# The messages of the tensor-product layer inside the first 100 turns of the ODE loop

## What is computed

```python
tpw = h @ W_mlp4 / jnp.sqrt(jnp.float32(W_mlp4.shape[0]))   # h: 64 numbers an edge
w1, w2, w3, w4 = jnp.split(tpw, 4, axis=-1)
s0 = x0[sender]; s1 = x1[sender]
p1 = w1 * s0 * y0
p2 = (w2 * s0)[:, :, None] * y1[:, None, :]
p3 = w3[:, :, None] * s1 * y0[:, None, :]
p4 = w4 * jnp.einsum('eum,em->eu', s1, y1) / SQRT3
msg0 = jax.ops.segment_sum(jnp.concatenate([p1, p4], axis=-1), receiver, num_segments=num_nodes)
msg1 = jax.ops.segment_sum(jnp.concatenate([p2, p3], axis=1), receiver, num_segments=num_nodes)
```

```python
f = lambda z: _mlp(z, *params)           # tanh, tanh, linear
k1 = f(y)
k2 = f(y + dt / 2 * k1)
k3 = f(y + dt / 2 * k2)
k4 = f(y + dt * k3)
return y + dt * (k1 + 2 * k2 + 2 * k3 + k4) / 6
```

## Time and profile before

| | |
|---|---|
| median of 3 runs | 7954.03 us (7952.38 to 7956.33) |
| the profiled execution | 7959.73 us |
| its span | 7958.1 us |
| TensorE busy | 6785.0 us, 85% of the span, 208683 matmuls |
| VectorE busy | 2457.7 us, 31% |
| ScalarE busy | 1713.8 us, 22% |
| GpSimd busy | 697.0 us, 9% |

### The profile page before, as it was taken

How to read it: one execution, slowest core, us unless ns; L and a number is a source line. 1 busy time by engine, 2 the same in 40 slices (tenths; PEclk the granted TensorE clock), 3 DMA queues, 4 the chain that set the end, 5 groups by cost and what they waited for, 6 DMA issues and landing times. The chain is left out here.

```text
span 7958.1 us, 480626 instructions
## 1 busy us (share of the span) xinstructions
PE 6785.0 (85%) x208683; PEld 3933.2 (49%) x208683; DVE 2457.7 (31%) x12720; ACT 1713.8 (22%) x7668; POOL 697.0 (9%) x1191
## 2 busy tenths in 40 slices
PE   7889989999999999999888888888888888888741
PEld 5423244444444444444487555555555555555520
DVE  5257643211111111111133222222222222222247
ACT  0223222333333333333100111111111111111111
POOL 0034359200000000000000000000000000000000
PEclk9889989999999999999899999999999999999975
DMA  1133211000000000000032111111111111111100
GB/s 42 22 85 89 79 53 50 8 0 0 0 0 0 0 0 0 0 0 0 12 120 71 6 6 6 6 7 6 6 6 6 6 6 7 7 6 6 20 12 7
DMA packets 739824, 152.53 MB, mean 19 GB/s; under 512 B 694067, under 2 KB 708981, under 8 KB 739756
## 3 DMA queue, kind: packets, MB, share of 16 engines
q1 hardware_dynamic: 695596, 85.27, 7.2%
q0 software_dynamic: 40704, 45.90, 2.1%
q10 hardware_dynamic: 3456, 20.48, 0.6%
HBM read 123.19 MB, written 28.16 MB: 19 GB/s over the span
## 5 line engine op out<-in xcount | busy, mean ns | idle before, releaser
L988 PE MATMUL ode_busy<-ode_busy_x,ode_busy_w 128*32 128x320 f16 (+2 forms) x40000 | 2344.2, 311 | 44.5 <-issue 37.6
L1461 PE MATMUL ps_rows<-whh,h_pair 128*4 128x384 f16 x34944 | 1554.1, 327 | 149.7 <-DVE h_pair L1361 146.1
L1461 PEld LDWEIGHTS ps_rows<-whh,h_pair 128*4 128x4 f16 x34944 | 746.1, 84 | 774.0 <-DVE h_pair L1361 212.9
L982 PEld LDWEIGHTS ode_psa<-ode_a,ode_w2t 128*32 128x32 f32 x19968 | 411.5, 108 | 734.1 <-ACT ode_a L1037 578.0
L988 PEld LDWEIGHTS ode_busy<-ode_busy_x,ode_busy_w 128*32 128x32 f16 x40000 | 712.4, 95 | 58.2 <-issue 58.1
L1410 ACT COPY gate_rows<-ps_rows 128x384 f32<-128x384 f32 x624 | 298.3, 478 | 1982.4 <-PE ps_rows L1461 1982.4
L1373 DVE COPY gate_rows<-ps_rows_last 128x128 f32<-128x128 f32 x624 | 181.9, 292 | 1715.2 <-PE ps_rows_last L1461 1715.2
L1039 ACT ACTIVATE ode_b<-ode_psa 128x1 f32<-128x1 f32 x2496 | 427.3, 171 | 951.4 <-PE ode_psa L982 951.4
L982 PE MATMUL ode_psa<-ode_a,ode_w2t 128*32 128x1 f32 x19968 | 602.7, 180 | 0.0
L1037 ACT ACTIVATE ode_a<-ode_psu 128x1 f32<-128x1 f32 x1872 | 320.2, 171 | 729.8 <-PE ode_psu L982 729.8
L982 PE MATMUL ode_psa<-ode_ones,ode_b_parts 128*32 128x1 bf16 x9988 | 457.8, 163 | 0.0
(11 more groups left out here) (430 smaller groups left out, 8534.5 us busy)
## 6 DMA issues: line engine op xcount, KB each, us to landing
xg_buf<-xg_scratch SPq DMA_DIRECT2D x1248, 16.0 KB, 2.0
split_raw<-in_whh_t SPq DMA_DIRECT2D x32, 512.0 KB, 3.3
ig_w<-in_wih_t SPq DMA_DIRECT2D x8, 2048.0 KB, 10.6
xg_scratch<-ig_out ACTq DMA_DIRECT2D x16, 832.0 KB, 4.1
xg_scratch<-ig_out ACTq DMA_DIRECT2D x8, 836.0 KB, 3.6
msg_h<-h_scratch SPq DMA_DIRECT2D x88, 62.5 KB, 2.7
h_scratch<-mlp_h SPq DMA_DIRECT2D x40, 125.0 KB, 2.3
msg_snd<-up_scratch,msg_idx POOLq DMA_INDIRECT x176, 5.5
```

Source lines behind the costliest of these rows:

```text
L982: m = nc.tensor.matmul(ps[32 * j:32 * j + 32, 0:1], w[:, 32 * j:32 * j + 32], col, start=start, stop=stop, skip_group_check=True)
L988: nc.tensor.matmul(ps_busy[32 * j:32 * j + 32, 0:cols], busy_w[:, 32 * j:32 * j + 32], busy_x[:, 0:cols], start=True, stop=True, skip_grou ...
L1461: m = nc.tensor.matmul(out[32 * j:32 * j + 4, :], hpair[:, c, 2 - 2 * part:6 - 2 * part], whh[:, at + lo:at + hi], start=(part == 0 and c ...
```

## The change

The messages of all nodes are made inside the first SHADOW = 100 turns of the ODE loop, but for the units with an edge of node 0, which are made ahead of it.

- A unit is now two edge tiles, 250 edges, and there are 80. The graph stage has RING = 2 buffers for 4, and its votes find a sixth first and count: the units with an edge of node 0.
- `stage_jobs` (new, VectorE alone, 68 linked instructions on one partition) makes tables of jobs: for each turn its unit, the node tile whose receivers it counts and the place its sum is added to. A turn without a job has receivers out of range and adds zeros. Where there are more than 99 jobs, the rest stand ahead of the loop.
- `stage_first_messages` (new) does node 0's jobs: `edge_products` makes an edge tile's message with VectorE alone (the three pieces of p2 too), TensorE adds up two tiles in PSUM, and `add_messages` adds the sum to the buffer `messages` in SBUF. The output product of node 0's tile (`fout`) gives `x_first`, from which the ODE starts.
- In each of the first 100 turns, of 24 slots for filling, 18 hold pieces of a job in place of zeros: 6 of the sum of tile 0, 3 of the weights of tile 1, then 3 of zeros, 6 of the sum of tile 1, 3 of the weights of the next job's tile 0, 3 of zeros. A piece is a third of 512 columns in f32 (172, 170 and 170), as four quarters of 32 partitions (the last of 29). The weights' product reads 128 rows where it read 64; the added ones are zeros.
- A step has six slots where it had eight: `zh` and `zf` come from ScalarE, right behind the tanh of `a` and of `b`. VectorE's `p` is no longer an operand of TensorE; three more products with `mt_third` and `mt_sixth` take its place, in two of the slots that fell away.
- A turn's VectorE works in the order: sum of step 0, message of tile 0, sums of steps 1 and 2, the two adds of the last job, message of tile 1, sum of step 3.
- A second loop does turns 100 to 155 with zeros in all slots, and the splitting of weights stands beside that one, in pieces of 512 columns for 1024, since the message buffers now lie in `whh`. The output product of all five tiles (`mout`) comes behind the ODE.

The core of the diff:

```diff
-UNIT = 4 * TE
+UNIT = 2 * TE
...
+SHADOW = 100
+JOBS = NT * UNITS
+FIRST_JOBS = UNITS + JOBS - (SHADOW - 1)
...
-    RING = 4
+    RING = UT
...
+def add_messages(nc, v, S, msg, acc, i, offset):
+    v.wait_ge(S["acc"], i + 1)
+    for b in range(2):
+        part = msg[:, ds(offset + b * BANK, BANK)]
+        last = nc.vector.tensor_tensor(part, acc[b][0:TN, :], part, ALU.add)
+    last.then_inc(S["added"], 1)
...
+        THIRDS = ((0, 172), (172, 342), (342, BANK))
+        def sum_piece(pe, i, a, b, third):
+            lo_col, hi_col = THIRDS[third]
+            if (a, b, third) == (0, 0, 0):
+                pe.wait_ge(M["added"], i + 1)
+                pe.wait_ge(M["vec"], i * UT + 1)
+            for lo, hi in NODE_QUARTERS:
+                m = nc.tensor.matmul(acc[b][lo:hi, lo_col:hi_col], B["hot"][a][:, lo:hi], B["m"][a][:, b * BANK + lo_col:b * BANK + hi_col],
+                                     start=(a == 0 and third == 0), stop=(a == UT - 1), skip_group_check=True)
+            if (b, third) == (1, 2):
+                m.then_inc(M["acc" if a else "summed"], 1)
...
+        def job_slot(pe, i, n, cols):
+            if n < 6:
+                sum_piece(pe, i, 0, n // 3, n % 3)
+            elif n < 9:
+                if n == 6:
+                    pe.wait_ge(M["vec"], i * UT + 2)
+                    pe.sem_inc(M["ready"], 1)
+                weight_piece(1, n - 6)
+            elif 12 <= n < 18:
+                sum_piece(pe, i, 1, (n - 12) // 3, n % 3)
+            elif 18 <= n < 21:
+                if n == 18:
+                    pe.wait_ge(M["vec"], i * UT + (UT + 1))
+                    pe.sem_inc(M["ready"], 1)
+                    pe.wait_ge(M["h3_in"], i * 16 + 32)
+                    pe.sem_inc(M["ready"], 1)
+                weight_piece(0, n - 18)
+            else:
+                busy(cols)
+        def steps_tensor(pe, i, fill):
+            for r in range(UN):
+                k = i * (4 * UN) + 4 * r
+                b = b_col[r]
+                for s in range(4):
+                    fill(6 * r + (0, 2, 3, 4)[s], BUSY_A)
+                    pe.wait_ge(S["a"], k + (s + 1))
+                    quarters(ps_a, w2t, a_col[:], False, True).then_inc(S["wa"], 1)
+                    if s == 0:
+                        pe.wait_ge(S["zb"], i * (2 * UN) + (2 * r + 1))
+                        quarters(ps_u, ident, zh[:], True, False)
+                        fill(6 * r + 1, BUSY_B)
+                    elif s == 1:
+                        quarters(ps_u, ident, zh[:], True, False)
+                        pe.wait_ge(S["zb"], i * (2 * UN) + (2 * r + 2))
+                        quarters(ps_z, m0_parts, ones16[:], False, False)
+                        quarters(ps_z, mt_sixth, b[:, 0:1], False, False)
+                    elif s == 2:
+                        quarters(ps_u, ident, zf[:], True, False)
+                        quarters(ps_z, mt_third, b[:, 1:2], False, False)
+                    else:
+                        quarters(ps_z, mt_third, b[:, 2:3], False, False)
+                        fill(6 * r + 5, BUSY_B)
+                    pe.wait_ge(S["b"], k + (s + 1))
+                    if s < 3:
+                        quarters(ps_u, mt_full if s == 2 else mt_half, b[:, s:s + 1], False, True).then_inc(S["wu"], 1)
+                    else:
+                        quarters(ps_z, mt_sixth, b[:, 3:4], False, True).then_inc(S["wz"], 1)
...
+        def steps_scalar(a, i):
+            for r in range(UN):
+                for s in range(4):
+                    if s == 0:
+                        a.wait_ge(S["wz"], i * UN + (r + 1))
+                        nc.scalar.activation(a_col[:], ps_z[:, 0:1], ACT.Tanh).then_inc(S["a"], 1)
+                        nc.scalar.activation(zh[:], ps_z[:, 0:1], ACT.Identity, bias=m0h[:]).then_inc(S["zb"], 1)
+                        a.wait_ge(S["out"], i * UN + (r + 1))
+                    else:
+                        a.wait_ge(S["wu"], i * (3 * UN) + (3 * r + s))
+                        nc.scalar.activation(a_col[:], ps_u[:, 0:1], ACT.Tanh).then_inc(S["a"], 1)
+                    a.wait_ge(S["wa"], i * (4 * UN) + (4 * r + s + 1))
+                    nc.scalar.activation(b_col[r][:, s:s + 1], ps_a[:, 0:1], ACT.Tanh).then_inc(S["b"], 1)
+                    if s == 0:
+                        nc.scalar.activation(zf[:], ps_z[:, 0:1], ACT.Identity, bias=m0f[:]).then_inc(S["zb"], 1)
...
+                with v.Fori(0, SHADOW) as i:
+                    tile, column = table_load(v, table, 0, i, ET - UT), table_load(v, table, 1, i, NT * TN)
+                    offset = table_load(v, table, 2, i, (NT - 1) * 1024)
+                    step_sum(v, i, 0)
+                    v.wait_ge(M["summed"], i + 1)
+                    edge_products(nc, v, M, snd_in, B, ps_w, i, 0, tile, column)
+                    step_sum(v, i, 1)
+                    step_sum(v, i, 2)
+                    add_messages(nc, v, M, msg, acc, i, offset)
+                    edge_products(nc, v, M, snd_in, B, ps_w, i, 1, tile, column)
+                    step_sum(v, i, 3)
...
-    PIECE = 1024
+    PIECE = 512
```

More of the change, by code:

```diff
@@ L693, in _ @@
             def _(sp):
-                first, count = bound(sp, j, 0, first_max), bound(sp, NT + j, 1, count_max)
-                with sp.Fori(0, count) as i:
-                    unit = nc.s_assert_within(first + i, 0, first_max, skip_runtime_bounds_check_because="first + count is at most the number of units")
-                    for b in range(T // 2):
-                        sp.wait_ge(S["tpw"], i * T + (2 * b + 2))
-                        sp.dma_start(h3[b][:], h3_dram[:, ds(unit * UNIT + b * (2 * TE), 2 * TE)]).then_inc(h3_in[b], 16)
+                with sp.Fori(0, bound(sp)) as i:
+                    tile = table_load(sp, first_table, 0, i, ET - UT)
+                    sp.wait_ge(S["tpw"], i * UT + UT)
+                    sp.dma_start(B["h3"][0:HIDDEN, :], h3_dram[:, ds(tile * TE, UNIT)]).then_inc(S["h3_in"], 16)
@@ L702, in _ @@
             @block.gpsimd
             def _(g):
[L704 to L714 removed]
+                with g.Fori(0, bound(g)) as i:
+                    load_edges(nc, g, S, snd_in, B, up_dram, i, table_load(g, first_table, 0, i, ET - UT))
@@ new lines, in _ @@
+                v.wait_ge(S["cleared"], 1)
+                v.sem_inc(S["vec"], UT)
+                v.sem_inc(S["added"], 1)
+                with v.Fori(0, bound(v)) as i:
+                    tile, column = table_load(v, first_table, 0, i, ET - UT), table_load(v, first_table, 1, i, NT * TN)
+                    offset = table_load(v, first_table, 2, i, NT * 1024)
+                    for a in range(UT):
+                        edge_products(nc, v, S, snd_in, B, ps_w, i, a, tile, column)
+                    add_messages(nc, v, S, msg, acc, i + 1, offset)
@@ L812, in _ @@
             def _(pe):
-                for i in range(NT):
+                for i, t in enumerate(tiles):
                     for b in range(2):
@@ L973, in _, with quarters @@
                 v.wait_ge(S["made"], 3)
-                link(nc.vector.tensor_copy(ramp[:], ramp_i[:]))
+                link(nc.vector.tensor_copy(ramp[:], ramp_i))
                 link(nc.vector.tensor_scalar(ramp[:], ramp[:], DT, None, ALU.mult))
+        def quarters(ps, w, col, start, stop):
+            for j in range(4):
+                m = nc.tensor.matmul(ps[32 * j:32 * j + 32, 0:1], w[:, 32 * j:32 * j + 32], col, start=start, stop=stop, skip_group_check=True)
+            return m
```

527 lines of the change are left out of this document (294 added, 233 removed).

## The result

The changed kernel takes 7713.57 us (median of 4, 7704.82 to 7742.18) against 7955.18, a ratio of 0.970 (95%: 0.968 to 0.973). It is faster, by 242 us, where 532 were forecast; 7713 lies above the range (7375 to 7620). Its profiled execution took 7742.18 us, 217.5 less than the one of before.

What follows compares the result with a forecast made beforehand. Stage lengths on one core bound it, the ODE loop by its TensorE-ScalarE chain. Terms -595.7 - 44 + 60 + 10.6 + 24 + 13 = -532 from 7959.73 gave 7427.6, median 7422 us; 8-in-10 range 7375 to 7620.

Steps and rivals of the forecast that it cites:

- the clock falls: Rival, ODE loop: two fills a step gone, TensorE drops to 1.2 GHz, some 4.6 us a turn over 156 turns: 8130; 3%.
- The sign of being wrong: A first-loop turn passing 18.5 us (pieces or VectorE), or a second-loop turn passing 18 (clock or GpSimd).
- Pieces hidden, all quarters side by side: ODE turns: four f32 products stream together, a piece takes 0.31 us, under the 0.42 and 0.39 windows, costing nothing; 79%.
- two at a time: Rival, ODE turns: f32 pieces overlap only twofold, 0.58 us each, 306 us in all: 7728; 8%.
- staircase: Rival, ODE turns: a quarter's two passes stand in a row, 0.72 us a piece, 560 us in all: 7982; 4%.
- A turn of 17.5 us: First ODE loop: 17.53 - 0.12 from the chain + 0.1 for added waits, over 100 turns with messages.
- The second loop, 17.38 us: 56 ODE turns without messages: 17.53 - 0.15 us each, with the weight splitting beside them.
- The graph stage, +13, bounds 0 and 30: Graph stage with two buffers for four: a round of 1.15 us for two tiles, net +13 us.
- First messages, output product, tables: Added work: node 0's messages 60 us, their output product 10.6, job tables with the number row 24.
- VectorE late: Rival, ODE turns: VectorE's instructions grow beside gathers and pieces wait, perhaps 2 us a turn: 7620; 4%.

Runs made afterwards that it cites:

- e9: The changed kernel with the weights' product reading 64 rows instead of 128: 8110.05 us, ratio 1.019.
- e5: The changed kernel with two rounds of four 192-column zero quarters in stages 1 and 2 of the first loop's steps only: 7525.28 us, ratio 0.946.
- e13: The changed kernel with 128 rows in the sum's products too, the added three being zeros: 7616.61 us, ratio 0.958.
- e6: e5 without the gathers in the first loop, each indirect DMA replaced by an increment of its semaphore: 7504.72 us.
- e14: e7 with one round of four 384-column zero quarters in stages 1 and 2 in both loops: 7482.98 us, ratio 0.942.
- e7: The changed kernel with four one-hot buffers in the graph stage, its loop taking two units at a time: 7693.45 us, ratio 0.967.
- e1: The changed kernel with its f32 pieces multiplying zeros by zeros: 7864.63 us.
- e11: The changed kernel with each piece as two rounds of four f16 zero products of 344 (340) columns, second run: 7552.02 us.
- e15: The changed kernel with two rounds of four 192-column zero quarters in stages 1 and 2 in both loops, second run: 7907.28 us.

## Why the prediction was wrong

The step that failed is the rival "the clock falls", which I gave 3% with the words that the LSTM keeps a granted clock of 1.00 with TensorE busy 83%. Busy share was the wrong measure: in the changed loop TensorE is busy 93% at a clock of 0.76, in e9 96% (1638.68 of 1700) at 0.52. I had looked at the zeros as time to be covered, and not as what holds the clock. The earlier trace rows had a hint that I passed by: a clock of 0.97 in the first part of the loop, where TensorE waited longer between its zeros. In size the rival was right where it applied: 17.5 + 4.6 = 22.1 us a turn at the lower level, measured 22.8; but it holds for a part of the first 100 turns and not for all 156. Its reason was half of it: the two idle slots a step are in the second loop too, which has f16 zeros in all its other slots and keeps 0.98. It takes the f32 pieces beside them, 12 of 18 with 125 rows, to bring the clock to 0.76; filling the slots (e5: 1.00) or giving the pieces 128 rows (e13: 0.89) each brings it back, wholly or in part. Cost: 2021.8 - 100 x 18.04 = 218 us; e5 took 208 of them back. The sign of being wrong came true (a turn of the first loop took 20.2 us, over 18.5), but I had put pieces or VectorE beside it and not the clock.

The other steps:

- *Pieces hidden, all quarters side by side.* Right. Eight records in 0.47 to 0.50 us, and neither "two at a time" nor "staircase" is seen. The Trainium skill (TensorE: Matmul & The Clock Gate, Part 3) has matmuls start and end in strict program order; by my reading of it a piece would have taken 0.72 us. The trace has the records of the piece at 1167.94 start in two groups, four within 0.02 us and the other four 0.15 us later, so a quarter's two passes do not stand in a row.
- *A turn of 17.5 us.* Measured 18.04, 54 us in all. The waits ahead of pieces 0, 6 and 18 cost 0.11 + 0.05 + 0.29 = 0.45 us a turn by the intervals between ScalarE's activations (0.93 for 0.82 at the edge, 0.58 and 0.82 for 0.53), where I took 0.1 of "0 to 0.4". The two waits in a row ahead of piece 18 are the dear ones. The other 0.25 is the activation that is late beside the gather; e6 shows it to be the gather's. I had asked only what waits for GpSimd; nothing in the ODE's chain does, and ScalarE is slowed all the same.
- *The second loop, 17.38 us.* Right: 17.36 where the clock holds. It falls now and then (0.98), 6 us in all; e14 has 17.35 throughout.
- *The graph stage, +13, bounds 0 and 30.* Mis-sized, and outside its bounds: 140.5 us for its tiles, +48.5. I priced a round of two buffers at 1.15 us. The timeline of VectorE there has 1.56, and it waits for TensorE at every round:

```profile
60.48 0.39 DVE L224 TENSOR_SCALAR hot_s<-iota_h,src_f 125x625 f16<-125x625 f16 x1 [0.47 <-PE ps_adj L276]
...
61.32 0.25 DVE L225 TENSOR_SCALAR hot_d<-iota_h,dst_f 125x125 f16<-125x125 f16 x1
62.04 0.39 DVE L224 TENSOR_SCALAR hot_s<-iota_h,src_f 125x625 f16<-125x625 f16 x1 [0.47 <-PE ps_adj L276]
62.34 0.25 DVE L225 TENSOR_SCALAR hot_d<-iota_h,dst_f 125x125 f16<-125x125 f16 x1
62.58 0.39 DVE L224 TENSOR_SCALAR hot_s<-iota_h,src_f 125x625 f16<-125x625 f16 x1
62.65 1.15 PEld L276 LDWEIGHTS ps_adj<-hot_d,hot_s 125*125 125x125 f16 x10 [0.41 <-DVE hot_d L225]
```

  The two engines take turns: the next one-hots start 62.04 - 60.48 = 1.56 after the last, since TensorE's products follow the one-hots of the same buffer and the semaphore comes back only then. My round counted one tile's products and one hand-over. By the rows VectorE idles 0.47 us a round and TensorE's weight loads 0.41; how that divides between a second hand-over and the loop's edge is not shown. e7 and e14, with four buffers, give 43 to 45 us of it back.
- *First messages, output product, tables.* 60, 10.8 and 23.5 us for 60, 10.6 and 24. The first 60 agrees because of the 10 us set aside for a cold TensorE: without it the stage took 2 us more ahead of the jobs, 3 more in their four cycles (11.2 to 12.5 us each from the second on, for 10.4) and 5 more behind them, at a granted clock of 0.72.
- *VectorE late.* Did not come: the pieces' waits are "issue", none is for VectorE.

The forecast of faster was right, and the range was too narrow above: it left the clock out. Of the 315 us by which the profiled sums differ (532 and 217) 280 are the ODE loop and 35 the graph stage.

## What to carry to other kernels

Before you take zero matmuls away or put real ones in their place, ask what they hold up besides time: a product with fewer rows or less streaming, or an idle slot that looks free, can drop TensorE's clock, and busy share will not show it; the granted clock in a window will. Padding a contraction to 128 rows with zeros cost nothing here at full clock (the product behind a piece starts 0.42 us after it with 64, 125 or 128 rows). Three rows of zeros in 12 of 18 pieces were worth 97 us; 64 in the other 6 were worth 396, part of it through longer turns at the lower level. And count a loop's instructions, not only its time: a fill with fewer and wider matmuls did the same for the clock (e14: 1.00 in both loops).

## What the runs showed of the hardware

- The granted clock of the first loop went with the rows that its pieces read: 64 rows in 6 of 18 pieces and 125 in the other 12 gave 0.52 (e9, whose turns are also longer), 125 rows in 12 and 128 in 6 gave 0.75 to 0.80, 128 rows in all 0.88 to 0.89. Zeros or numbers as operands made no difference.
- f32 quarters of 172 columns stream four side by side, 0.47 to 0.50 us for eight records with their tail, 0.77 at 1.2 GHz. At 1.2 GHz a piece of 64 rows held the product behind it for 0.72 us and one of 128 rows for 0.55, at 2.4 GHz both for 0.42 (e9 and the changed kernel); why is open.
- While GpSimd issues an indirect DMA (1.22 us), ScalarE's next activation can be late by 0.25 us (gone in e6, which has no gathers), and on one chip by 1.0 us (e1). With f16 pieces (e11) the gathers were there and the 0.25 us was not; what is shared is open.
- A loop of 560 matmuls a turn (e15) fetched some four packets of instructions a turn and took 24.6 us a turn at a clock of 0.83; with 528 (e14) it fetched none and took 17.35 at 1.00.
